# A slot-ordered state-space and ternary-MLP kernel: every engine's order inside a slot rewritten

## The reference, cut to what matters

```python
u  = silu(conv4(in_proj(ctx)) + b)               # per batch: 512 channels x 512 steps
dt, B, C = split(x_proj(u)); dt = softplus(dt_proj(dt))
state = state * exp(dt * A) + (dt * u) * B_t     # over 512 steps, 16 states a channel
y  = sum_n(state * C_t) + D * u
x  = x + tanh(g_x) * y * silu(layernorm(x))      # x is rows x columns: y is turned
h  = silu(bitlinear(layernorm(x), w1)) * bitlinear(layernorm(x), w2)     # 2048 wide
x  = x + tanh(g_f) * bitlinear(h, w3)
# bitlinear: rmsnorm, quantise a row to 127 levels of its peak, weights to -1, 0, 1
```

## Time and profile before

| | |
|---|---|
| median of 3 runs | 708.96 us (707.74 to 710.83) |
| the profiled execution's own time | 708.85 us |
| its span, first to last instruction | 707.1 us |
| POOL busy | 602.3 us |
| DVE busy | 598.6 us |
| ACT busy | 523.3 us |
| PE busy | 513.7 us |
| mean granted TensorE clock | 0.891 |

### The profile page before, as it was taken

The page is one execution under the profiler, slowest core; times in us unless marked ns, Lnnn a source line. Parts: engine busy times, 40 slices in busy tenths (PEclk is TensorE's granted clock), DMA queues, the critical chain, the costliest instruction groups (busy, mean ns, idle before and its releaser), DMA issues.

```text
span 707.1 us, 8143 instructions
## 1 busy us (share of the span) xinstructions
PE 513.7 (73%) x2562; PEld 315.4 (45%) x2562; DVE 598.6 (85%) x842; ACT 523.3 (74%) x980; POOL 602.3 (85%) x295
## 2 busy tenths in 40 slices
PE   9787889883446639777566577677686777758897
PEld 3243444433443426454544345355453544445554
DVE  7679768877997998989958998998889989888865
ACT  5754867599987647868686787798798797677654
POOL 1499899999999959799998999898998999888421
PEclk9899999998567969899685889899999999989999
DMA  5696875499910000146400000035520000000001
GB/s 171 217 403 218 309 297 191 152 331 405 357 61 6 30 1 15 60 161 211 165 20 1 30 0 16 1 132 211 193 76 1 15 2 16 0 15 17 1 16 45
DMA packets 23930, 80.78 MB, mean 114 GB/s; under 512 B 2432, under 2 KB 4608, under 8 KB 20816
## 3 DMA queue, kind: packets, MB, share of 16 engines
q1 hardware_dynamic: 23888, 80.27, 30.9%
HBM read 72.53 MB, written 7.73 MB: 114 GB/s over the span
## 4 chain that ended last, share of the span: by engine, by line
DVE 30%; ACT 27%; PE 20%; issue 11%; POOL 7%; DMA 3%; SPq 1%; DVEq 0%; ACTq 0%
DVE hh L767 8%; ACT da L730 7%; DVE hh L764 4%; POOL hh L812 3%; PE bank_t L1138 3%; POOL hh L704 3%; PE bank_y L845 3%; PE bank_b L1000 3%; PE bank_a L994 3%; DMA wq<-x 2%; DVE sm L1060 2%; ACT room L1035 2%; ACT room L1149 2%; ACT room L1014 2%; ACT da L737 2%
## 5 line engine op out<-in xcount | busy, mean ns | idle before, releaser
L767 DVE TENSOR_TENSOR_SCAN hh<-da,hh 128x1024 f32<-128x1024 f32 x91 | 206.5, 2279 | 10.7 <-POOL hh L704 6.7
L845 PE MATMUL bank_y<-ident,hh 128*128 128x128 f32 x1024 | 147.3, 294 | 20.4 <-POOL hh L812 16.2
L845 PEld LDWEIGHTS bank_y<-ident,hh 128*128 128x128 f32 x1024 | 131.4, 154 | 51.6 <-POOL hh L812 25.5
L807 POOL TENSOR_TENSOR hh<-hh,cc 128x1024 f32<-128x1024 f32 x62 | 146.1, 2357 | 4.0 <-ACT hl L749 2.9
L812 POOL TENSOR_TENSOR hh<-hh,cc 128x1024 f32<-128x1024 f32 x61 | 143.6, 2354 | 0.0
L704 POOL TENSOR_TENSOR hh<-pair,bb 128x1024 f32<-128x1024 f32 x30 | 70.7, 2358 | 26.7 <-DMA bb<-xd_scratch 24.9
L698 POOL TENSOR_TENSOR hh<-wq,bb 128x1024 f32<-128x1024 f32 x32 | 75.3, 2354 | 12.4 <-PE bank_y L845 12.4
L704 POOL TENSOR_TENSOR hh<-wq,bb 128x1024 f32<-128x1024 f32 x32 | 75.3, 2352 | 11.9 <-PE bank_y L845 11.7
L764 DVE TENSOR_TENSOR_SCAN hh<-da,hl,hh 128x256 f32<-128x256 f32 x128 | 85.2, 729 | 0.0
L698 POOL TENSOR_TENSOR hh<-pair,bb 128x1024 f32<-128x1024 f32 x32 | 75.4, 2357 | 9.1 <-PE bank_y L845 9.1
L730 ACT ACTIVATE da<-wq,cst 128x256 f32<-128x256 f32 x128 | 53.3, 466 | 12.8 <-DVE hh L764 12.7
(11 more groups left out here) (256 smaller groups left out, 1042.3 us busy)
## 6 DMA issues: line engine op xcount, KB each, us to landing
bb<-xd_scratch SPq DMA_DIRECT2D x32, 512.0 KB, 5.1
cc<-xd_scratch SPq DMA_DIRECT2D x32, 512.0 KB, 6.8
wq<-weights SPq DMA_DIRECT2D x12, 1024.0 KB, 6.7
stage<-weights SPq DMA_DIRECT2D x8, 1024.0 KB, 6.1
xin<-x SPq DMA_DIRECT2D x4, 1024.0 KB, 5.2
room<-weights SPq DMA_DIRECT2D x4, 1024.0 KB, 8.5
u_scratch<-wq SPq DMA_DIRECT2D x6, 512.0 KB, 3.1
wq<-x SPq DMA_DIRECT2D x2, 1024.0 KB, 18.2
```

What stands on the lines that cost most here:

```text
L767: ins = v.tensor_tensor_scan(to, da, h, 0.0, ALU.mult, ALU.add)
L807: ins = g_.tensor_tensor(quarters(flat(hh[k % NH])), quarters(flat(hh[k % NH])), cc[:, n:n + 4, t], ALU.mult)
L845: mm = pe.matmul(bank_y[:, (first + c) * P:(first + c + 1) * P], flat(hh[k % NH])[:, at:at + P], ident[:, :], start=False, stop=(s == STEP ...
```

## The change

Instructions and their shapes stay nearly the same; their order inside a slot changes on PE, DVE, ACT and POOL. These parts stand out.

- PE: `ab_tensor` is split into its first product (`a_tensor`) and its second (`b_tensor`), and `ht_tensor` calls stand before and between them instead of behind. `out_tensor` is made in two halves, with `front_tensor` between. Transposes of rows and of gates come earlier in the slot.
- ACT: a piece of weights is rounded first in its slot, ahead of `tanh` and `exp`. `hq_scalar` and `center_scalar` come right after `exp`, and the copies of turned quarters are spread over the slot.
- DVE: scales, statistics, peaks and `z_vector` change places.
- POOL: the two small powers for the rows (`rstd`, `cfac`) come after `times_c`, not ahead of it.
- Group 4 of the gate goes straight to x2, and `gate_late` is gone.
- `c_by_vector` becomes 14, 45, 53, 63, 77. ACT rounds five pieces of the weights instead of four. Two pairs, one gate slot and some rounding slots move by one. `center_scalar` and the statistics ahead of it move one slot later.
- After the loop a few calls change places.

```diff
-PAIR = {2: 25, 3: 37, 4: 49, 5: 66, 6: 87, 7: 99}
+PAIR = {2: 26, 3: 37, 4: 49, 5: 65, 6: 87, 7: 99}
+BY_VECTOR = (14, 45, 53, 63, 77)
 def c_by_vector(k):
-    return k % STEPS == 5 and 40 < k < 80
+    return k in BY_VECTOR
...
-            if g == NE:
-                YV.did(v.tensor_tensor(gbuf[:, q, :], bank_y[:, :], gbuf[:, q, :], ALU.mult), ("y", g))
-                return
             YV.did(v.tensor_tensor(bank_y[:, :], bank_y[:, :], gbuf[:, q, :], ALU.mult))
...
-            if g == NE + 1:
+            if g == NE:
                 v.wait_ge(*WA.of(("sign", NW - 1)))
...
-        def gate_late(v, g):
-            v.wait_ge(*WA.of(("sign", NW - 1)))
-            v.wait_ge(*YV.of(("y", g)))
-            YV.did(v.tensor_tensor(columns(x2[1], 0), by_rows(gbuf[:, 0, :]), columns(xin, 0), ALU.add))
...
-            return (20, 21, 23, 24, 25, 26, 28, 29, 30, 31, 33, 34)[i]
+            return (20, 21, 23, 24, 25, 26, 28, 29, 30, 32, 33, 35)[i]
...
-            return i in (1, 4, 7, 10)
+            return i in (0, 3, 7, 9, 10)
...
+        def chunk_before(i, c):
+            if i == END and c == 1:
+                return (-1, 0)
+            if at_end(i):
+                return (i, c - 2) if c >= 2 else (i - 1, c + 2) if i > END else (i - 1, NCH - 1)
+            return (i, c - 1) if c else (i - 1, NCH - 1)
...
 # POOL, slot k
+                    if k < ALL and not c_by_vector(k):
+                        times_c(g_, k)
+                    for i in range(END):
+                        if k == tile_slot(i) + 7:
+                            rh_pool(g_, i)
                     if k == 10:
                         g_.wait_ge(*ZA.of("var"))
...
-                    if k < ALL and not c_by_vector(k):
-                        times_c(g_, k)
...
 # ACT, slot k, its first statement
+                    for i in range(NW):
+                        if k == round_slot(i) and rounded_by_scalar(i):
+                            weight_round_scalar(act, i)
...
 # PE, slot k, after sums, rows, pairs and gates
+                        if k == tile_slot(i) + 10:
+                            out_tensor(pe, i, (0, 1))
+                    for b in (1, 2, 3):
+                        front_tensor(pe, b, k)
...
+                        if k == tile_slot(i) + 10:
+                            out_tensor(pe, i, (2, 3))
+                        if k == tile_slot(i) + 9:
+                            ht_tensor(pe, i, 2)
+                        if k == tile_slot(i) + 8:
+                            ht_tensor(pe, i, 0)
+                        if k == tile_slot(i) + 9:
+                            ht_tensor(pe, i, 3)
+                            a_tensor(pe, i, c)
+                        if k == tile_slot(i) + 8:
                             ht_tensor(pe, i, 1)
-                            ht_tensor(pe, i, 2)
-                            ht_tensor(pe, i, 3)
+                            b_tensor(pe, i, c)
...
 # DVE, slot k, its last statement
-                    if k == PER + 3 * NE:
-                        gate_late(v, NE)
...
 # PE, after the loop
-                out_tensor(pe, 13)
                 ab_tensor(pe, 15, 0)
                 ab_tensor(pe, 15, 1)
+                out_tensor(pe, 13)
```

More of the change, by code:

```diff
@@ L970, in xqt_scalar, with a_tensor @@
                                   bias=nmagic), ("xqT", i))
-        def ab_tensor(pe, i, c):
-            a, b_ = bank_ab(i, c)
+        def chunk_before(i, c):
[4 more added lines that the diff above has]
+            return (i, c - 1) if c else (i - 1, NCH - 1)
+        def a_tensor(pe, i, c):
+            a, before = bank_ab(i, c)[0], chunk_before(i, c)
             if c == 0:
@@ L996, in ab_tensor, with b_tensor @@
             MP.did(mm, ("a", i, c))
+        def b_tensor(pe, i, c):
+            b_, before = bank_ab(i, c)[1], chunk_before(i, c)
             if before[0] >= 0:
@@ L1160, in out_tensor @@
                 pe.wait_ge(*WA.of(("sign", NW - 1)))
-            if i >= END:
+            if i >= END and 0 in groups:
                 pe.wait_ge(*MV.of(("out", i - 1)))
@@ L1407, in _ @@
                         y_keep(act, k // STEPS - 1)
+                    for first, n, done in TURNS:
+                        if k == done + 3:
+                            center_scalar(act, first, n)
+                    for i in range(END):
+                        if k == tile_slot(i) + 7:
+                            hq_scalar(act, i, 0)
+                            hq_scalar(act, i, 1)
                     for b in (1, 2, 3):
                         front_scalar(act, b, k)
-                        if k == FRONT[b] + 9:
-                            x_dbl_scalar(act, b)
+                    for i in range(0, NW, 2):
+                        if k == sum_slot(i):
+                            weight_sum(act, i)
+                    if k == 9:
+                        variance_scalar(act)
                     for i in range(NW):
[L1413 to L1416, removed]
                         if k == sign_slot(i):
                             weight_sign(act, i)
-                    for first, n, done in TURNS:
-                        if k == done + 2:
-                            center_scalar(act, first, n)
                     for n in PAIR:
@@ L1540, in _ @@
                         if 0 <= c < NCH:
-                            ab_tensor(pe, i, c)
-                        if k == turned(i):
-                            ht_tensor(pe, i, 0)
+                            a_tensor(pe, i, c)
+                    for i in range(END - 1):
+                        if k == tile_slot(i) + 8:
                             ht_tensor(pe, i, 1)
-                        if k == turned(i) + 1:
-                            ht_tensor(pe, i, 2)
-                            ht_tensor(pe, i, 3)
+                    for i in range(END + 1):
+                        c = k - tile_slot(i)
+                        if 0 <= c < NCH:
+                            b_tensor(pe, i, c)
                 sums(pe, 124)
@@ L1624, in _ @@
                     for i in range(END):
+                        if k == tile_slot(i) + 7:
+                            scales_vector(v, i, 1)
+                    for i in range(END):
                         c = k - tile_slot(i) - 1
@@ L1635, in _ @@
                         scan(v, k + LEAD - 1)
-                        if c_by_vector(k + LEAD - 1):
-                            times_c_vector(v, k + LEAD - 1)
                     for b in (1, 2, 3):
                         front_vector(v, b, k)
+                    for first, n, done in TURNS:
+                        if k == done + 4:
+                            rows_vector(v, first, n)
                     for i in range(16):
@@ L1642, in _ @@
                             row_statistics(v, i)
+                    for i in range(END):
+                        if k == tile_slot(i) + 5:
+                            scales_vector(v, i, 0)
                     for n in PAIR:
@@ L1659, in _ @@
                                 aggr_vector(v, i)
-                        if k == done + 4:
-                            rows_vector(v, first, n)
+                    for i in range(END - 1):
+                        if k == tile_slot(i) + 10:
+                            out_vector(v, i)
+                    for i in range(NE):
+                        if k == z_turn_slot(i):
+                            y_first(v, i)
+                    if k + LEAD - 1 < ALL and c_by_vector(k + LEAD - 1):
+                        times_c_vector(v, k + LEAD - 1)
+                    for i in range(END):
+                        if k == tile_slot(i) + 4:
+                            peak_vector(v, i, 1)
+                    for i in range(1, NW, 2):
+                        if k == sum_slot(i):
+                            weight_sum_vector(v, i)
+                    for i in range(END):
+                        if k == tile_slot(i) + 2:
+                            peak_vector(v, i, 0)
                     for i in TILES:
```

101 lines of the change are left out of this document (43 added, 58 removed).

## The result

The changed kernel takes 675.67 us in the median of four executions (673.3 to 678.5), the kernel before 709.21 beside it. The ratio is 0.9528, with a 95% interval of 0.9485 to 0.9571. Forecast were 690.4 us and a range of 681 to 703: right in direction, 15 us short, and outside the range. Six more executions later (after_again) gave 676.53.

The account below looks back on a forecast made before the run. POOL was taken as the bound up to 258 us, and no single engine from 265 to 655, where DVE, ACT and PE keep each other waiting. Terms summing to -18.5 took 708.85 to 690.4 us, range 681 to 703.

Parts of the forecast that it names:

- The late add: Group 4's 512-column DVE add in slot 44 goes, and POOL's 7.51 us wait comes back: -7.5 us.
- Ends only when POOL's queue has run dry: Reading of the 8.21 us DVE add with two SBUF inputs: it lasts over three further POOL products.
- The head, four terms: Early slots: small power on POOL -1.9, step 14 off POOL -2.3, weights' lost head start +1.5, POOL's small gaps -1.0.
- The first two terms: Slot 10, times_c fills POOL's wait for variances, -1.9 us; step 14's product with C leaves POOL, -2.3 us.
- POOL's gaps: Two gaps between 84 and 258 us, both from PE coming late: -1.0 of 1.8 us.
- Steps 61 and 69 back, 63 away: Products with C in the long stretch: +2.3 us on POOL, -1.2 on DVE, half taken: +1.2 us.
- The order inside the slots: Long stretch, 265 to 655 us: new orders return one third of POOL's 25.7 us of waits on sums, -8.5 us.
- the outer bound: Fastest time allowed if the new order gains more than forecast: down to 675 us, chance 0.07.
- Behind the loop: After the loop, PE works without a pause and moving product 13 leaves its work as it is: 0 (±1) us.
- The order gives nothing: Rival: in the long stretch DVE takes over what PE gives back, only the sure terms remain: 698.9 us, chance 0.19.
- the stall comes back in slot 40: Rival: group 4's new add in slot 40 stalls too, from layout or xin: 697.9 us, chance 0.06.
- The loop around PE at +9: Rival: a_tensor behind the fourth quarter closes a loop of waits, 4.7 to 5.7 us per slot: 712 us, chance 0.06.

Follow-up runs that it names:

- after_again: The changed kernel executed again, unedited: 676.53 us in the median (675.7 to 678.3).
- b_gate: The kernel before with one edit, group 4 of the gate straight to its place in slot 40, no late add: 701.82 us.
- a_late: The changed kernel with the late add of group 4 put back in slot 44: 685.49 us, 9.5 us slower.
- a_two: The changed kernel plus one DVE add of two SBUF inputs, 64 columns, at the end of slot 44: 676.85 us.
- a_six: The changed kernel plus eight DVE adds of two SBUF inputs, 192 columns each, in slots 41 to 62: 690.06 us.
- a_pair: The changed kernel with the pair of batch 1 made in slot 25 again instead of 26: 677.49 us.
- a_tab: The changed kernel with the old tables (steps by DVE, pairs, gate and rounding slots, four pieces rounded by ACT), all orders as changed: 682.26 us.
- a_ab: The changed kernel with both products of the next tile ahead of the older tile's quarters on PE: 705.43 us, 30 slower.

## Why the prediction was right or wrong, point by point

- **The late add, -7.5.** The price was right: 7.2 us between steps 44 and 48, 7.5 there in b_gate's trace, 8.5 by b_gate's median, 9.5 by a_late's. "Ends only when POOL's queue has run dry" was wrong as a rule: a_two waited for one product. The Trainium skill's rule (SBUF — State Buffer, section "Who interferes with whom": two SBUF inputs on DVE contend with GpSimd's reads, the one that issues first holds the ports for its instruction) describes a_two and seven of a_six's eight adds. The adds of 8.21, 8.78 and 9.21 us it doesn't: in each POOL began three more products first. The two clusters of the kernel before, 8 to 9 us apart, are what one would see if the add sometimes gets its turn at once; no trace of the lower cluster was taken, so that is argued.
- **The head, four terms summing to -3.7.** 2.7 us at step 44 in one execution, 0.8 in the other; too much was forecast, by 1 to 3 us. The first two terms came: at step 20 the changed kernel is 4.5 us ahead (3.1 in after_again), against -1.9 and -2.3. POOL's gaps weren't closed as forecast: of the two in the earlier trace rows the later is gone, the earlier grew to 1.48 us, and a new one of 2.13 stands in slot 29, where PE waited for the first gate tile. a_pair shows that the pair in slot 26 isn't what decides.
- **Steps 61 and 69 back, 63 away, +1.2.** It can't be read alone. It is part of a_tab, where the new tables as a whole are worth 6 us; no run shows the term by itself.
- **The order inside the slots, -8.5.** This is the step that failed: the overlap was mis-sized by taking one third of the waits. With the term above, -7.3 was forecast for steps 48 to 127, and 22.5 to 25.7 came. The bound was right, 25.7 us of POOL's waits on sums; that one execution gained just this to the tenth is luck. (By the prediction's own terms the outer bound is 698.9 - 25.7 = 673.2, not 675.) The choice of one third was wrong: "DVE's own 342 us leave little room between the waits". DVE was busy 342 of 390, but POOL's floor for the same steps lay at 359 and DVE's below it. With 17 us between the two floors, there was room for all of it. What the sentence took for a second bound was idle time of an in-order list. The better orders and tables took most of POOL's away, busy 411.8 of 415 now, while DVE's work stayed what it was, 339.9 us from 258 to 623.5. Not every wait went: PE's for the gated product stands at 39.6 us.
- **Which order brings it.** The prediction named PE first, with the product between the quarters, and the ACT rounding second. Both are there (8 and 12 us when undone). ACT's part was seen only from PE's side: PE's 37.6 us were quoted and ACT's 30 us of waits for the same transposes were not. With all else in place ACT's order is the dearer one. That `exp` for the scan stands behind those waits is the likely reason; no run tried it apart. DVE's order and the tables brought 12 us on top of the other two, where the tables' terms summed to +0.4 and DVE's order had none of its own.
- **Behind the loop, 0.** Right: 48.0 us before and after, and in after_again.
- **The rivals.** "The order gives nothing" fell. So did "the stall comes back in slot 40": that add takes 0.69 us. The loop around PE at +9 rested on the misreading, since `a_tensor` had always stood behind the quarters. a_ab built the nearest real loop, and it cost 30 us.

## What to carry to other kernels

When one engine has a floor well under the span and its waits can be summed, take that sum as the bound on a better order's gain, and don't cut it down for an engine whose own busy time stays under that floor. Here nearly all of it came; that was one kernel. An engine with idle time between is not a bound. In a ping-pong between two in-order engines (transpose, copy, transpose, copy) put work of another tile between, on both sides: adjacent copies alone cost 11 us here. Then check which loop of waits is the longest, since one swap made it 5.9 us in place of 4.6. Read the old order off the timeline as well as off the source.

## What the runs showed of the hardware that had not been expected

A DVE add with two SBUF inputs, issued while POOL's products follow each other without a gap, took 0.92 us (64 columns), 0.49 to 2.43 us and once 9.21 (192 columns), and 8.21 and 8.78 us (512 columns). In the long cases POOL began three more products in the meantime, and the add ended 0.2 to 0.6 us after the last of them. In the seven short cases of a_six the POOL product that began while the add waited took 2.46 to 2.49 us, the others 2.34 to 2.37. An add of 512 columns with one input in PSUM took 0.69 us.
